# Graph network on one core: four parts of source-sorted rows instead of three, up to four sums beside a chunk of picks, no filler products

## What is computed

```python
src_h = h[src] @ W_msg.T + b_msg                                  # layer 0
messages = segment_sum(src_h + edge_embed[type], dst)
x = x + gru_cell(messages, h)
h = relu(layernorm(x))                                            # layer 1
agg = segment_sum(h[dst], src)
z = ((1 + eps) * h + agg) @ W1.T + b1
x = x + relu(batchnorm(z)) @ W2.T + b2
```

## Time and profile before

| | |
|---|---|
| runs | 4891.22, 4886.05, 4887.57 us; median 4887.57 us |
| the profiled execution | 4883.31 us, span 4881.0 us |
| PE, PEld, DVE, ACT, POOL busy | 77%, 54%, 55%, 33%, 71% |
| mean granted PE clock | 0.879 |
| gathers of layer 0 | from 150 us, all issued by 2246 us |
| scatters of layer 1 | 2467 to 4659 us |
| sums after the last scatter | 4668 to 4824 us |
| the two maps and the output | 4824 us to the end |

### The profile page before, as it was taken

One profiled execution on the slowest core, in us unless ns is written; L12 is line 12 of the kernel. 1 busy time (PEld: TensorE's weight loads), 2 busy tenths in 40 slices (PEclk: granted clock), 3 DMA queues, 4 the chain that ended last, 5 costly groups with the idle time before them and its releaser, 6 DMA issues.

```text
span 4881.0 us, 93192 instructions
## 1 busy us (share of the span) xinstructions
PE 3759.2 (77%) x22928; PEld 2659.4 (54%) x23224; DVE 2671.9 (55%) x4808; ACT 1613.8 (33%) x3340; POOL 3442.0 (71%) x3576
## 2 busy tenths in 40 slices
PE   4698888888888888888787777777677775677457
PEld 3455555555555555556654444444466674667456
DVE  7777777777777777756821111111255552555267
ACT  4433333333333333333432222222222222222266
POOL 1577777777777777774167777777777777777763
PEclk8799988989899888999998999988888886788689
DMA  5332333333333221222222222222355553555365
GB/s 151 98 82 80 80 81 81 81 80 81 81 80 81 64 53 53 53 52 55 75 92 81 81 85 81 81 86 81 125 182 177 186 185 125 167 174 185 103 240 159
DMA packets 316351, 514.65 MB, mean 105 GB/s; under 512 B 73350, under 2 KB 231737, under 8 KB 300189
## 3 DMA queue, kind: packets, MB, share of 16 engines
q1 hardware_dynamic: 209245, 286.59, 18.6%
q0 software_dynamic: 106944, 226.05, 15.7%
HBM read 331.72 MB, written 180.64 MB: 105 GB/s over the span
## 4 chain that ended last, share of the span: by engine, by line
POOL 66%; issue 24%; PE 4%; DVE 2%; DMA 1%; POOLq 1%; ACT 1%; SPq 0%; ACTq 0%; DVEq 0%
POOL rows_by_src L692 34%; POOL sb_ring L662 31%; PE ps L1777 2%; DMA rows_by_src<-sb_cf 0%; PE ps L1797 0%; PE ps L1789 0%; POOL sb_oh L677 0%; DVE sb_stepE L966 0%; POOLq L157 0%; DMA rows_by_src<-sb_ring,sb_idxslot 0%; DVE sb_smalls L945 0%; ACT sb_ring L731 0%; DVE sb_stepE L969 0%; POOLq L689 0%; POOLq L153 0%
## 5 line engine op out<-in xcount | busy, mean ns | idle before, releaser
L692 POOL DMA_INDIRECT rows_by_src<-sb_ring,sb_idxslot x1664 | 1693.6, 1018 | 537.6 <-issue 503.8
L662 POOL DMA_INDIRECT sb_ring<-msg_table,sb_idxslot x1664 | 1584.9, 952 | 516.6 <-issue 504.1
L1593 PE MATMUL ps<-sb_zeros_b 128*128 128x512 bf16 x5465 | 1461.8, 416 | 105.2 <-issue 94.0
L1593 PEld LDWEIGHTS ps<-sb_zeros_b 128*128 128x128 bf16 x5760 | 580.8, 106 | 726.5 <-issue 284.2
L1733 PE MATMUL ps<-sb_H,sb_oh 128*128 x3520 | 616.1, 338 | 459.0 <-ACT ps L867 275.3
L1733 PEld LDWEIGHTS ps<-sb_H,sb_oh 128*128 128x128 f32 x3520 | 567.1, 245 | 562.3 <-issue 547.8
L1373 DVE TENSOR_SCALAR sb_oh<-sb_oh,sb_cf 128x512 f32<-128x512 bf16 x440 | 208.4, 501 | 1081.0 <-PE ps L1733 977.8
L791 ACT CAST sb_counts<-ps 54x512 bf16<-54x512 f32 x440 | 254.3, 578 | 1307.4 <-PE ps L1615 1294.8
L873 ACT CAST sb_ring<-sb_skeyE 128x4 f32 (+1 forms) x416 | 82.2, 198 | 1594.1 <-DMA rows_by_src<-sb_ring,sb_idxslot 1592.2
L1601 PEld LDWEIGHTS ps<-sb_ring,sb_oh 128*128 128x128 f32 x3520 | 504.5, 201 | 159.3 <-issue 95.9
L1601 PE MATMUL ps<-sb_ring,sb_oh 128*128 x3520 | 529.1, 292 | 41.4 <-SPq L476 41.1
(11 more groups left out here) (239 smaller groups left out, 4348.1 us busy)
## 6 DMA issues: line engine op xcount, KB each, us to landing
sb_stepE<-rows_by_src SPq DMA_DIRECT2D x110, 1088.0 KB
sb_oh<-step_targets SPq DMA_DIRECT2D x110, 512.0 KB, 3.9
rows_by_src<-sb_cf SPq DMA_DIRECT2D x588, 68.0 KB
sb_ring<-msg_table,sb_idxslot POOLq DMA_INDIRECT x1664
rows_by_src<-sb_ring,sb_idxslot POOLq DMA_INDIRECT x1664
sb_ring<-rows_by_src SPq DMA_DIRECT2D x15, 1088.0 KB, 5.1
msg_table<-sb_oh SPq DMA_DIRECT2D x14, 448.0 KB, 3.3
sb_oh<-in_x SPq DMA_DIRECT2D x49, 128.0 KB, 2.1
```

Of the source, the lines that this page charges most:

```text
L662: pool.indirect_dma_start(out=ring[:, r * G + q, 0:F], out_offset=None, in_=table_d[:, :], in_offset=bass.IndirectOffsetOnAxis(ap=idxslot[ ...
L692: pool.indirect_dma_start(out=rows_d[:, :], out_offset=bass.IndirectOffsetOnAxis(ap=idxslot[:, h, g * G + q:g * G + q + 1], axis=0), in_=r ...
L1593: mm(o, zeros_b[:, 0:P], zeros_b[:, :], start=False, stop=True, skip_group_check=True)
```

## The change

`PASSES` becomes 896, 384, 256 and 128 batches, so `SCHUNKS` becomes 63, 31, 23 and 15: 117 sums lie beside the picks (94 before), 15 come after the last scatter (31 before), 132 in all (125 before). `SUM_RATE` gives each part its sums at a pair of chunks of picks: 6 for the first (three after each chunk), 4 for the second, 8 for the third (four after each chunk). In chunks of picks: the first part's sums lie at chunks 64 to 84 (three each), the second's at 88 to 103 (two each), the third's at 104 to 109 (four each, the last one three). Both kinds of filler go. DVE reads the offsets of a sum just ahead of its keys, no longer those of both sums ahead of the picks. The residual is loaded in pieces of ten blocks, forty blocks in each of the first two turns of the last loop, and `b2` is added ten blocks at a time in all four slots. `sum_blocks` goes through the steps in two halves, and the count tables take two parts in one bank and two in another.

```diff
-FILL_0, FILL_1 = 8, 10
-B2_CUTS = (0, 5, 10, BLOCKS // FIN)
-PASSES = (768, 512, 384)
+PASSES = (896, 384, 256, 128)
+SUM_RATE = (6, 4, 8)
+XB = 10
+XLAST = (BLOCKS - (FBODIES - 1) * RSLOTS * XB) // (FCH - FBODIES * RSLOTS)
+XPIECES = 16 * -(-BLOCKS // XB)
+XPARTS = (FBODIES - 1) * RSLOTS + FCH - FBODIES * RSLOTS
...
-        plan.append((a, a + 1, s, 4))
-        full = n // 4
-        plan.append((a + 1, a + full, s + 4, 4))
+        plan.append((a, a + 1, s, rate, rate))
+        full = n // rate
+        plan.append((a + 1, a + full, s + rate, rate, rate))
...
             def picks_and_sums(j, k, sums, first, own):
-                offs = [group_offsets(s, sumrow, (regs, regs_o)[i]) for i, (s, h) in enumerate(sums)]
                 layer1_pick(j, k)
                 if own:
                     own_rows(j * 2 + k, k)
+                offs = []
                 for i, (s, h) in enumerate(sums):
+                    offs.append(group_offsets(s, sumrow, (regs, regs_o)[i % 2]))
                     for g in range(GPC):
                         sum_keys(s, h, g)
                         if i:
-                            sum_add(sums[0][0], g, offs[0])
+                            sum_add(sums[i - 1][0], g, offs[i - 1])
...
-            def fin_in(i):
-                sp.dma_start(H[:, ds(i * FINW, FINW)].rearrange("p (b f) -> p b f", f=F),
-                             x1v[:, ds(i * (BLOCKS // FIN), BLOCKS // FIN), :]).then_inc(S("fin_x"), 16)
+            def fin_in(i, n=RSLOTS * XB):
+                for a in range(0, n, XB):
+                    w = min(XB, n - a)
+                    sp.dma_start(H[:, ds(i * (RSLOTS * XB * F) + a * F, w * F)].rearrange("p (b f) -> p b f", f=F),
+                                 x1v[:, ds(i * (RSLOTS * XB) + a, w), :]).then_inc(S("fin_x"), 16)
...
+                cuts = (0, SS // 2, SS)
...
                 for z in range(NPASS):
-                    link(vs.tensor_reduce(part_s, tmp, axis=AX.X, op=ALU.add))
+                    for a, b in zip(cuts, cuts[1:]):
+                        link(vs.tensor_reduce(part_s[:, a:b], tmp, axis=AX.X, op=ALU.add))
...
                     pe.wait_ge(S("agg_zero"), n + 1)
-                    keep_warm(bank(1 + g), FILL_0)
                     wait_tiles("tiles_in", n)
...
-                    if alone:
-                        keep_warm(bank(7), FILL_1)
                     wait_tiles("bank_clear", n)
...
+            pe.wait_ge(S("bank_free"), OV * GPC)
             nc.tensor.sem_inc(S("sum_done"), 2 * GPC)
```

More of the change, by code:

```diff
@@ L96, in pick_phases @@
     turns = TURNS // 2
-    plan, at = [(0, 1, None, 0), (1, turns, None, 0), (turns, turns + 1, None, 0)], turns + 1
+    plan, at = [(0, 1, None, 0, 0), (1, turns, None, 0, 0), (turns, turns + 1, None, 0, 0)], turns + 1
     for z in range(NPASS - 1):
         a = -(-(-(-(TILES_BY[z] + BLOCKS) // CH)) // 2)
-        plan.append((at, a, None, 0))
-        s, n = FIRST_C[z], SCHUNKS[z]
-        plan.append((a, a + 1, s, 4))
-        full = n // 4
-        plan.append((a + 1, a + full, s + 4, 4))
+        assert at <= a
+        plan.append((at, a, None, 0, 0))
+        s, n, rate = FIRST_C[z], SCHUNKS[z], SUM_RATE[z]
+        plan.append((a, a + 1, s, rate, rate))
+        full = n // rate
+        plan.append((a + 1, a + full, s + rate, rate, rate))
         at = a + full
-        if n % 4:
-            plan.append((at, at + 1, s + full * 4, n % 4))
+        if n % rate:
+            plan.append((at, at + 1, s + full * rate, n % rate, rate))
             at += 1
-    plan.append((at, PAIRS, None, 0))
+    assert at <= PAIRS
+    plan.append((at, PAIRS, None, 0, 0))
     return [p for p in plan if p[1] > p[0]]
@@ L362, in pick_loop @@
         def pick_loop(engine, body, unrolled=0):
-            alone = min(p[0] for p in PICK_PHASES if p[3])
-            for a, b, s0, n in PICK_PHASES:
+            for a, b, s0, n, rate in PICK_PHASES:
                 def pair(j):
                     for k in range(2):
-                        sums = [((j - a) * 4 + s0 + i, (s0 + i) % 2) for i in range(2 * k, min(2 * k + 2, n))] if n else []
+                        half = rate // 2
+                        sums = [((j - a) * rate + s0 + i, (s0 + i) % 2) for i in range(half * k, min(half * k + half, n))] if n else []
                         own = b <= TURNS // 2 or (b == TURNS // 2 + 1 and k < TURNS % 2)
-                        body(j, k, sums, s0 if j is a and k == 0 and s0 in FIRST_C else "alone" if b <= alone else None, own)
+                        body(j, k, sums, s0 if j is a and k == 0 and s0 in FIRST_C else None, own)
                 if b - a == 1 or b <= unrolled:
@@ L595, in _, with next_rows @@
             fin_in(0)
-            with sp.Fori(1, FBODIES) as j:
+            def next_rows(j):
                 for r in range(RSLOTS):
@@ L599, in _ @@
                     rows_in(j * RSLOTS + r, r)
+            with sp.Fori(1, FBODIES - 1) as j:
+                next_rows(j)
                 fin_in(j)
+            next_rows(FBODIES - 1)
+            fin_in(FBODIES - 1, BLOCKS - (FBODIES - 1) * RSLOTS * XB)
             for r in range(FCH - FBODIES * RSLOTS):
@@ L1423, in add_b2 @@
                 if r == 0:
[L1424 to L1426 removed]
+                    dve.wait_ge(S("fin_x"), XPIECES if isinstance(i, int) and i == FBODIES - 1 else i * 64 + 64)
+                w = XLAST if isinstance(i, int) and i == FBODIES - 1 else XB
+                v = H[:, ds(i * (RSLOTS * XB * F) + r * w * F, w * F)].rearrange("p (b f) -> p b f", f=F)
                 vs.tensor_tensor(v, v, b2_blocks.to_broadcast([P, w, F]), ALU.add).then_inc(S("b2_added"), 1)
@@ L1441, in layer1_sum @@
                     vs.tensor_tensor(yb, yb, bank(r % 2 * GPC + g), ALU.add).then_inc(S("bank_free"), 1)
-                if r < RSLOTS - 1 and not (isinstance(j, int) and j == 0):
+                if not (isinstance(j, int) and j == 0):
                     add_b2(j - 1, r)
             dve.wait_ge(S("picked"), GROUPS)
+            dve.wait_ge(S("sum_done"), (OV + 2) * GPC)
             nc.vector.sem_inc(S("bank_free"), 2 * GPC)
@@ L1588, in rel @@
                                           skip_runtime_bounds_check_because="consecutive steps' blocks differ by 0 or 1")
-            def keep_warm(o, count):
-                for _ in range(count):
-                    mm(o, zeros_b[:, 0:P], zeros_b[:, :], start=False, stop=True, skip_group_check=True)
             def sum_rows(g, k, n):
@@ L1716, in _, with picks @@
             picked_ps = ps[:, 0:GPC, :].rearrange("p a b -> p (a b)")
-            def picks(j, k, alone, own):
+            def picks(j, k, own):
                 c = j * 2 + k
@@ L1750, in picks_and_sums @@
             def picks_and_sums(j, k, sums, first, own):
-                picks(j, k, first == "alone", own)
+                picks(j, k, own)
                 if first == 0:
```

17 lines of the change are left out of this document (9 added, 8 removed).

## The result

The changed kernel takes 4906.9 us (median of 8), the kernel before 4891.0 us on the same chip. The ratio is 1.0031 with a 95% interval of 1.0020 to 1.0042: slower by more than the 0.2% that can be told from no change. The number lies in the range, but I had forecast 4890 us and no change. One of the eight runs of the changed kernel took 5064 us at a lower granted clock (0.558 against 0.66) and is left out of the ratio. The profiled execution took 4907.5 us (span 4905.4), its mean granted clock was 0.659.

A forecast was written before the change was run, and what follows sets the result against it. POOL's issue rate for 1664 gathers and 1664 scatters was taken as the bound. Terms −75 + 74 − 4 + 4 + 3 = +2 us on the median 4887.6 gave 4890 us, no change; range 4848 to 4932.

The forecast's parts named there:

- Tail: After the last scatter: 16 fewer chunks of sums at 5.04 us save 80.6 us, less 6 given back: −75 us.
- the two give-backs: In the last loop: 3 us for `b2` on DVE in fewer chunks, 3 us for denser transfers.
- Chain of a chunk: PE and DVE work from picks to next picks: 26.0 us with three sums, 31.2 us with four.
- Picks and sums together: Scatter stage: POOL stalls 49 us in the first part, 5 in the third, plus 20 us slower scatters: +74 us.
- contention: Scatter stage: 23 more sums beside scatters, each slowing POOL 0.85 us through its row load: 20 us.
- the ring's lead: Scatter stage: rows picked in advance, six groups of 5.6 us, cover 33 us before POOL stalls.
- Start: Before the first scatter: one more padding chunk on SP's queue +4 us, a longer `sum_blocks` +3 us.
- Fillers: Removal is hidden in layer 0 behind the gathers; at the start of the picks it saves 4 us: −4 us.
- Rival 2: Scatter stage: two row buffers make third sums wait for their loads, 27 and 33 us a chunk: 4920 us, chance 0.22.
- Rival 1: Scatter stage: the third sum is no dearer than the second, chunk 25.1 us: 4867 us, chance 0.28.
- Rival 3: Layer 0: without fillers a chunk at low clock takes 19.4 us, behind the gathers: 4945 us, chance 0.08.
- the test that I had set: Scatter stage: wrong in its core if POOL's waits stay below 40 us or exceed 120, or the gathers' pace changes.

The follow-up runs named there:

- e3: Changed kernel with a third row buffer for the third sums of the first part, loads issued three sums ahead: 4859.9 us, 0.9932 of the kernel before.
- e10: Changed kernel with the offsets of a chunk's first two sums loaded ahead of the picks again: 4942.2 us, 1.0114 of the kernel before.
- e4: Changed kernel with the fixed padding chunks' transfers issued before SP waits for the table of last rows: 4890.1 us, 0.9995 of the kernel before.
- e2: Kernel before without its filler products, otherwise untouched: 4890.7 us, 1.0004 of the kernel before.
- e1: Changed kernel with both sets of filler products put back: 4911.6 us, 1.0037 of the kernel before.
- e8: Changed kernel with parts 768, 384, 256, 256, rates 4, 4, 6, five spare blocks and padding transfers issued first: 4825.8 us, 0.9876 of the kernel before.

## Why the prediction was right and wrong

**Tail, −75 us: right.** Measured −78.0. The transfers did not fill it: the two give-backs, 6 us in the forecast, came to less than 3.

**Chain of a chunk, 26.0 and 31.2 us: right to half a microsecond.** Measured 26.5 and 31.1. The missing half is in the third sum, from the end of the second's products to the end of its own: 6.5 us, not 6.1; and the 6.1 held 0.4 us that its own terms do not give (4410.7 + 4.3 + 1.05 is 4416.1, not 4416.5). The described mechanism, a third sum that starts late because its rows go into the first sum's buffer, is the one that e3 removes. "The gap to the next picks shrinks by 0.2 us only" compares with a chunk of two sums, and there it stands (4.1 us before, 4.0 now). But with three sums DVE runs late, and with the loads still ahead of the picks the gap is 5.4 us: e10 against the change shows 1.5 us a chunk. That the move of the loads also shortens scatters where POOL never stalls was in no term.

**Picks and sums together, +74 us: mis-sized, +93.** This is the step that failed. Its stalls were 54 us and are 125; its contention was +20 us and is −32. Both go back to one figure, the 0.85 us for each sum that I put down to its row load. I let POOL's time for a chunk grow with the sums, to 21.9 us, and compared the chain with that. But the cost falls on POOL at DVE's unbroken series, once a chunk at most, and not with each load; and beside a chain that is slower than POOL there are fewer such scatters (11). In the starved chunks a scatter takes 0.98 us and 0.305 us to the next: 15.1 × 1.285 = 19.4 us. So a chunk falls behind by 26.5 − 19.4 = 7.1 us, 142 us in 20 of them; 107 us were measured, which leaves 35. That this is so near the 33 counted on for the ring's lead is chance. At the start of the first chunk with three sums 29 tiles stood moved by ACT and not yet scattered by POOL, 37 us; but that chunk, 41.6 us long and in no term of mine, used eight of them, and 21 tiles, 27 us, were left for the 20 intervals. The rest is some 6 us of slower scatters before the ring was empty, and rounding.

The errors in stalls and in contention have opposite signs, so the net is off by 19 us only. It can be put down to 0.5 us in 20 chunks, 10 us, and to the third part's stalls, 18 us instead of 5; together that is 4 us too much, which I leave open. The lead was back in the third part, 28 tiles at its start, but its first chunk with sums took 41.8 us and used twelve of them, and this too was in no term.

**Start, +4 and +3 us: more than half missed.** The last gather ends 8.5 us later, not 4, and the first scatter came 9.6 us later, not 3. The landing was scaled and the issue on SP's queue was not (e4). `sum_blocks` was priced about right: between the last gather and the first scatter the change takes 2.4 us longer than e2 (211.4 against 209.0), both without fillers.

**Fillers: right in the main.** Layer 0 hid the low clock, and e1 and e2 agree. Of the −4 us at the start of the picks, −1.3 to −3.1 are shown.

**The rivals.** Rival 2, the row buffer, named 26.4 us as the point from which it decides, and the chunks stand at 26.5: the result, 4907 us, lies between it and the forecast. Rival 1 fell with the 1.65 us that PE waits ahead of the third sum. Rival 3 fell with the gathers' pace. By the test that I had set, POOL's waits above 120 us, the prediction is wrong in its core although its range held: they are 162 us. The sum was −78 + 93 + 10, or +24 us on the profiled execution (9.6 + 92.9 − 78.1), against my +2. That the total stayed in the range is luck in part: the price of contention was put on the wrong cause, and the error that this made in the stalls was nearly cancelled by the one in the scatters.

What the change did, taken apart: the tail gave 78 us; the three and four sums of a chunk took back 129 us (e10's scatter stage, 2332.2, against 2202.9); the move of the offset loads gave 36 of these back; the padding and `sum_blocks` cost 8 to 10 us; the fillers nothing.

## What to carry to other kernels

When work is moved from behind a stage into it, compare the longest chain of one iteration with the pace of the bounding engine when it is undisturbed, not with its average beside the old load; beyond that point every microsecond of chain is lost once the lead of the ring is used up. Move only as much as the iterations hold at that rate: e8 moved half as much of the tail as the change and kept it. And where an order of instructions frees one engine's queue, look at what another engine does in that moment, since two register loads at another place in DVE's queue were worth 27 us of the kernel's time, 22 of them in shorter scatters on POOL.

## What was not expected of the hardware

A scatter that runs beside an unbroken series of DVE one-hots takes 2.5 to 3.6 us in place of 0.97 and ends 0.83 to 0.85 us after the series (208 of 254 unbroken series, none of 285 with a pause). Loads of 1088 KB beside the scatters lengthen them by nothing (275 scatters, 0.966 us). The issue of the padding transfers occupies SP's queue for up to 4.2 and 4.5 us each. A mean granted clock of 0.65 against 0.88 changes nothing measurable in a kernel whose gathers and scatters are the bound (e2, 1.0004).
